# Wide attention as one pipeline over four passes, with whole fp32 scores and the softmax division ahead of the transpose

## What is computed

```python
qkv = (x @ w_qkv).reshape(b, n, 3, HEADS, DIM_HEAD)      # HEADS 16, DIM_HEAD 64, n 256
q, k, v = transpose(qkv, (2, 0, 3, 1, 4))
sim  = einsum('bhid,bhjd->bhij', q * DIM_HEAD ** -0.5, k)
attn = softmax(sim, axis=-1)
out  = einsum('bhij,bhjd->bhid', attn, v)
return merge_heads(out) @ w_out
```

## Time and profile before

| what | us |
|---|---|
| time, median of 3 (2217.66 to 2232.74) | 2226.12 |
| the profiled execution, its own time | 2226.03 |
| its span, first to last instruction | 2224.2 |
| its mean granted TensorE clock | 0.962 of 2.4 GHz |

### The profile page before, as it was taken

How to read it: one execution, slowest core, us unless ns; L and a number is a source line. 1 busy time by engine, 2 the same in 40 slices (tenths; PEclk the granted TensorE clock), 3 DMA queues, 4 the chain that set the end, 5 groups by cost and what they waited for, 6 DMA issues and landing times. The chain is left out here.

```text
span 2224.2 us, 25438 instructions
## 1 busy us (share of the span) xinstructions
PE 1951.9 (88%) x8468; PEld 1143.5 (51%) x8468; DVE 1607.6 (72%) x3009; ACT 893.5 (40%) x1871; POOL 563.4 (25%) x497
## 2 busy tenths in 40 slices
PE   5779999999999989988988789987888887888998
PEld 2346657777776755556766545542232232224555
DVE  4868875454545468866665588857999999996887
ACT  2125444343434354534544523334434353333322
POOL 2633220000000022221011000005767777760000
PEclk9989999999999989999999999988999999999999
DMA  5000000000000000010000000000000000000000
GB/s 221 1 0 1 1 1 1 1 1 1 1 1 1 1 1 1 1 38 1 1 1 1 1 0 1 0 0 15 3 12 1 15 1 15 1 0 0 1 1 19
DMA packets 9633, 20.20 MB, mean 9 GB/s; under 512 B 1056, under 2 KB 8224, under 8 KB 8608
## 3 DMA queue, kind: packets, MB, share of 16 engines
q1 hardware_dynamic: 9504, 18.59, 2.5%
HBM read 14.39 MB, written 1.05 MB: 7 GB/s over the span
## 5 line engine op out<-in xcount | busy, mean ns | idle before, releaser
L1773 POOL TENSOR_TENSOR ssm_hc<-ssm_h,ssm_cm 128x512 f32<-128x512 f32 x256 | 334.3, 1307 | 135.3 <-DVE ssm_h L1856 134.7
L1856 DVE TENSOR_TENSOR_SCAN ssm_h<-banks,ssm_dbx 128x512 f32<-128x512 f32 x256 | 309.6, 1210 | 2.3 <-DVE ssm_dbx L1848 2.3
L515 PE MATMUL banks<-ffn_x_high,up_high 128*128 128x512 f32 x544 | 289.3, 532 | 5.8 <-DVE ffn_p L1489 2.5
L1657 PE MATMUL banks<-ssm_hc,const 128*128 128x512 f32 x512 | 267.4, 604 | 12.2 <-DVE ssm_gated L1831 9.3
L550 POOL TENSOR_TENSOR x_norm<-x_centred,x_square 128x512 f32<-128x512 f32 x24 | 32.8, 1367 | 921.9 <-ACT x_square L545 921.4
L1748 ACT ACTIVATE banks<-banks,a_neg 128x510 f32<-128x510 f32 x256 | 167.2, 659 | 242.5 <-PE banks L1644 241.5
L516 PE MATMUL banks<-ffn_x_low,up_high 128*128 128x512 f32 x544 | 218.5, 402 | 0.0
L517 PE MATMUL banks<-ffn_x_high,up_low 128*128 128x512 f32 x544 | 218.4, 401 | 0.0
L1467 ACT ACTIVATE ffn_th<-banks 128x512 f32<-128x512 f32 (+1 forms) x136 | 81.2, 597 | 273.2 <-PE banks L517 228.2
L1848 DVE TENSOR_TENSOR ssm_dbx<-banks,ssm_bm 128x512 f32<-128x512 f32 x256 | 170.7, 667 | 19.2 <-PE banks L1647 18.6
L1644 PE MATMUL banks<-ssm_packed,half 96*128 96x510 bf16 x256 | 101.7, 397 | 71.8 <-DVE ssm_h L1856 64.7
(11 more groups left out here) (259 smaller groups left out, 3824.7 us busy)
## 6 DMA issues: line engine op xcount, KB each, us to landing
ssm_packed<-ssm_parts SPq DMA_DIRECT2D x48, 64.0 KB, 2.0
up_whole<-in_up SPq DMA_DIRECT2D x1, 2304.0 KB, 16.0
weights<-in_weights SPq DMA_DIRECT2D x1, 2048.0 KB, 21.4
up_whole<-in_up SPq DMA_DIRECT2D x1, 2048.0 KB, 7.9
const<-in_const SPq DMA_DIRECT2D x1, 1426.5 KB, 6.6
half<-in_half SPq DMA_DIRECT2D x1, 1408.0 KB, 10.1
weights<-in_weights SPq DMA_DIRECT2D x1, 1168.0 KB, 23.9
weights<-in_weights SPq DMA_DIRECT2D x1, 1152.0 KB, 11.2
```

Source lines behind the costliest of these rows:

```text
L515: pe.matmul(out, w_high, x_high, start=True, stop=False)
L1657: pe.matmul(k.bank[5][:], k.c("hot")[:, P - row:2 * P - row], hc[:, i % HOLD, :], start=(i % NP == 0), stop=(i % NP == NP - 1)).then_inc(s ...
L1773: pool.tensor_tensor(hc[:, i % HOLD, :], h[:, i % HOLD, :], cm[:, i // NP % 2, :], ALU.mult) \
L1856: dve.tensor_tensor_scan(h[:, n % HOLD, :], k.bank[DELTA[n % AHEAD]][:], dbx[:, n % AHEAD, :], 0.0, ALU.mult, ALU.add).then_inc(s["h"], 1)
```

## The change

`wide_attention` takes all four passes in one list of 64 slots.

- q and k are stored whole, in fp32, by ACT alone. `scores` makes one fp32 product for each t and m, t outside, so that neighbours in the list are of different heads.
- The exponential also writes the sum of each row (`den`). DVE takes the reciprocal (`invert`), and POOL multiplies `pin` by it in place, four instructions a slot (`rden`, `scaled`). `turn` waits for that. `pin` and the small tiles are threefold (`RING`).
- DVE makes both copies into `pt`.
- `weigh` has the operands exchanged: `va` without its 65th column is stationary (64 columns), `pt` moves (256 columns), and the two heads write partitions 0 to 63 and 64 to 127 of bank 6. So the result is channel by token and isn't transposed again. ACT copies it once per pair of slots into `ot`.
- `output(p)` is eight products in a row, in slot 2 of the next pass, ahead of `turn` there; `weigh` comes behind it in that slot and waits for the residual.
- PE's order in a slot is scores, projection, weigh, then norm or v product, then turn. The v products lie in slots 3 to 6 and 11 to 14 (four before the first slot), all copied by DVE from bank 7. The norm of the next pass lies in slots 7 and 8.

```diff
-def wide_attention(k, n, p):
+def wide_attention(k, tag):
...
     nc = k.nc
-    G, HP, tag = 2, H // 2, f"{n}p{p}"
-    s = k.semaphores(f"attend{p % 2}", ATTEND)
+    G, HP = 2, H // 2
+    NS = HP * NB
+    ALL = PASSES * NS
+    RING = 3
+    s = k.semaphores("wide", ["proj", "moved", "v", "v_in", "scores", "max", "probs", "rden", "scaled", "turned",
+                              "pt", "pv", "ot", "y", "done"] + PREP)
...
-        q, kk = ([sb(f"{name}_{part}", [P, 2, T], F32R) for part in ("high", "low")] for name in "qk")
-        va = sb("va", [P, NT, H, DB + 1])
-        pin = sb("pin", [P, 2, 2, T])
+            return ctx.enter_context(nc.sbuf_tensor(f"wide_{name}", shape, dt))
+        q, kk = sb("q", [P, 2, T]), sb("k", [P, 2, T])
+        va = sb("va", [P, NT, H, DB])
+        pin = sb("pin", [P, RING, 2, T])
         pt = sb("pt", [P, 2, 2, T])
-        low = sb("low", [P, 2, 4])
-        rden = sb("rden", [P, 2, 2])
-        on = sb("on", [P, NT, H, DB])
-        ot = sb("ot", [P, 2, T])
+        low, den, rden = sb("low", [P, RING, 4]), sb("den", [P, RING, 4]), sb("rden", [P, RING, 4])
...
-        out = k.bank[6][:, 0:4 * (DB + 1)].rearrange("p (t m e) -> p t m e", t=2, m=2)
...
             def scores(i):
-                g, b = stages[i]
-                pe.wait_ge(s["k_low"], g + 1)
+                p, g, b = pair_of(i)
+                pe.wait_ge(s["moved"], 2 * (i // 2) + 2)
                 if i >= 2:
                     pe.wait_ge(s["probs"], i - 1)
                 else:
-                    pe.wait_ge(s["v_act"], NT)
-                    pe.wait_ge(s["v_dve"], NT)
-                for m in range(2):
-                    r = slice(64 * m, 64 * m + 64)
-                    for t in range(2):
-                        ins = cut_product(pe, k.bank[2 * (i % 2) + m][:, t * L:(t + 1) * L],
-                                          [part[r, g % 2, b * L + t * P:b * L + (t + 1) * P] for part in q],
-                                          [part[r, g % 2, b * L:(b + 1) * L] for part in kk])
+                    pe.wait_ge(s["v_in"], 4)
+                r = i // 2 % 2
+                for t in range(2):
+                    for m in range(2):
+                        rows = slice(64 * m, 64 * m + 64)
+                        ins = pe.matmul(k.bank[2 * (i % 2) + m][:, t * L:(t + 1) * L],
+                                        q[rows, r, b * L + t * P:b * L + (t + 1) * P],
+                                        kk[rows, r, b * L:(b + 1) * L], start=True, stop=True)
                 ins.then_inc(s["scores"], 1)
             def turn(i):
-                pe.wait_ge(s["probs"], i + 1)
+                pe.wait_ge(s["scaled"], i + 1)
                 if i >= 1:
-                    pe.wait_ge(s["pt_act"], i)
-                    pe.wait_ge(s["pt_dve"], i)
+                    pe.wait_ge(s["pt"], i)
                 for m in range(2):
                     for key in range(2):
                         for t in range(2):
                             ins = pe.transpose(k.bank[4 + m][:, key * L + t * P:key * L + (t + 1) * P],
-                                               pin[:, i % 2, m, t * L + key * P:t * L + (key + 1) * P], k.c("ident"))
+                                               pin[:, i % RING, m, t * L + key * P:t * L + (key + 1) * P], k.c("ident"))
                 ins.then_inc(s["turned"], 1)
...
             def weigh(i):
-                g, b = stages[i]
-                pe.wait_ge(s["pt_act"], i + 1)
...
-                for m in range(2):
-                    for t in range(2):
-                        for key in range(2):
-                            ins = pe.matmul(out[:, t, m, :], pt[:, i % 2, m, key * L + t * P:key * L + (t + 1) * P],
-                                            va[:, 2 * b + key, 2 * g + m, :], start=(key == 0), stop=(key == 1))
+                p, g, b = pair_of(i)
+                pe.wait_ge(s["pt"], i + 1)
+                pe.wait_ge(s["v_in"], 8 * p + 4 * (g // 4) + 4)
+                if b == 0 and i >= 2:
+                    pe.wait_ge(s["ot"], i // 2)
+                if i % NS == 0 and p >= 1:
+                    pe.wait_ge(s["done"], p)
+                for key in range(2):
+                    for m in range(2):
+                        ins = pe.matmul(k.bank[6][64 * m:64 * m + 64, b * L:(b + 1) * L], va[:, 2 * b + key, 2 * g + m, :],
+                                        pt[:, i % 2, m, key * L:(key + 1) * L], start=(key == 0), stop=(key == 1))
                 ins.then_inc(s["pv"], 1)
-            for i in range(NS + 2):
-                if i < NS:
+            def output(p):
+                pe.wait_ge(s["ot"], HP * (p + 1))
+                for g in range(HP):
+                    ins = pe.matmul(k.bank[6][:], k.w(G, "wout")[:, g * P:(g + 1) * P], ot[:, g, :],
+                                    start=(g == 0), stop=(g == HP - 1))
+                ins.then_inc(s["y"], 1)
...
+                p, at_slot = i // NS, i % NS
+                if i < ALL:
                     scores(i)
-                    if i + 3 < NS:
-                        project((i + 3) // 2, (i + 3) % 2)
-                if 1 <= i <= NS:
+                if i + 3 < ALL:
+                    project(i + 3)
+                edge = i >= NS + 2 and (i - 2) % NS == 0
+                if edge:
+                    output(p - 1)
+                elif i >= 2:
+                    weigh(i - 2)
+                if at_slot == 7 and p + 1 < PASSES:
+                    norm(p + 1, 0)
+                if at_slot == 8 and p + 1 < PASSES:
+                    norm(p + 1, 1)
+                if 11 <= at_slot < 15 and p + 1 < PASSES:
+                    values(8 * (p + 1) + at_slot - 11, 7)
+                if 3 <= at_slot < 7 and p < PASSES:
+                    values(8 * p + 4 + at_slot - 3, 7)
+                if 1 <= i <= ALL:
                     turn(i - 1)
-                if i >= 2:
+                if edge:
                     weigh(i - 2)
...
         @block.scalar
         def _(act):
             act.wait_ge(k.loaded, 16)
...
+                part, r = (q, kk)[n % 2], n // 2 % 2
+                act.wait_ge(s["proj"], n + 1)
+                if n >= 4:
+                    act.wait_ge(s["scores"], 2 * (n // 2) - 2)
+                act.activation(part[:, r, :], k.bank[7][:], ACT.Copy,
+                               scale=float(DB) ** -0.5 if n % 2 == 0 else 1.0).then_inc(s["moved"], 1)
...
+                if i + 3 < ALL:
+                    move(i + 3)
+                if i < ALL:
                     act.wait_ge(s["max"], i + 1)
-                    if i >= 2:
-                        act.wait_ge(s["turned"], i - 1)
+                    if i >= RING:
+                        act.wait_ge(s["turned"], i - RING + 1)
                     for m in range(2):
                         for t in range(2):
-                            cols = slice(t * L, (t + 1) * L)
-                            ins = act.activation(pin[:, i % 2, m, cols], k.bank[2 * (i % 2) + m][:, cols], ACT.Exp,
-                                                 bias=low[:, i % 2, 2 * m + t:2 * m + t + 1])
+                            cols, n = slice(t * L, (t + 1) * L), 2 * m + t
+                            ins = act.activation(pin[:, i % RING, m, cols], k.bank[2 * (i % 2) + m][:, cols], ACT.Exp,
+                                                 bias=low[:, i % RING, n:n + 1],
+                                                 accum_out=den[:, i % RING, n:n + 1])
                     ins.then_inc(s["probs"], 1)
...
+                if at_slot == 7 and p + 1 < PASSES:
+                    prepare_scalar(k, act, s, p + 1, 0)
+                if at_slot == 8 and p + 1 < PASSES:
+                    prepare_scalar(k, act, s, p + 1, 1)
+                if i >= 2 and i % 2 == 1:
+                    pair = (i - 2) // 2
+                    act.wait_ge(s["pv"], i - 1)
+                    if pair >= HP:
+                        act.wait_ge(s["y"], pair // HP)
+                    act.activation(ot[:, pair % HP, :], k.bank[6][:], ACT.Copy).then_inc(s["ot"], 1)
...
+        @block.gpsimd
+        def _(pool):
+            prepare_gpsimd(k, pool, s, 0)
+            for i in range(ALL):
+                pool.wait_ge(s["rden"], i + 1)
+                for m in range(2):
+                    for t in range(2):
+                        n, part = 2 * m + t, pin[:, i % RING, m, t * L:(t + 1) * L]
+                        ins = pool.tensor_scalar(part, part, rden[:, i % RING, n:n + 1], 1.0, ALU.mult, ALU.mult)
+                ins.then_inc(s["scaled"], 1)
+                if i % NS == 8 and i // NS + 1 < PASSES:
+                    prepare_gpsimd(k, pool, s, i // NS + 1)
...
+            def invert(i):
+                dve.wait_ge(s["probs"], i + 1)
+                dve.reciprocal(rden[:, i % RING, :], den[:, i % RING, :]).then_inc(s["rden"], 1)
+            for j in range(NT):
+                values(j, j)
```

(17 more changed lines are left out.)

## The result

| what | before | after |
|---|---|---|
| time, median, us | 2221.9 | 2139.35 |
| lowest to highest, us | 2215.97 to 2232.74 | 2135.41 to 2140.0 |
| span of the profiled execution, us | 2224.2 | 2133.6 |

The ratio is 0.962, with a 95% interval of 0.958 to 0.966: the change makes the kernel 3.8% faster; the medians lie 83 us apart. The forecast was 2127, in a range from 2104 to 2178.

What follows compares the result with a forecast made beforehand. PE bounded the layer (423 of 449 us busy); afterwards the ring would bound plain slots, PE those with v. Head, slots, v products, norms, edges and tail gave 344.5 us, plus clock 349.5 against 448.6: 2127 us, range 2104 to 2178.

Steps and rivals of the forecast that it cites:

- 63 steps at the plain slot: Steps from first to last turn in the wide attention layer, each taken at 4.25 us: 267.8 us.
- 28 v products, beyond a plain slot: Slots with an added v product, taken at 4.85 us, 0.60 more than a plain slot: 16.8 us.
- norms: The next pass's norm woven into the slots, holding back the projection by some 1.7 us a pass: 5 us in all.
- three edges: At each pass edge the output products stand before turn and weigh waits for the residual: 7.0 us each, 21.
- last turn to the end: The layer's tail: transposes, copies, last weigh, eight output products and residual, 12.2 us.
- clock: Mean clock of 0.97 loses some 10 us of PE work in the layer, half of it counted: 5 us.
- Scores and weigh: On PE, half arrays overlap fully in both products: 0.87 us each per slot, against 1.75 if serial.
- the prediction's first rival: Weigh's column halves do not overlap, so PE takes 0.88 us more a slot: 45 us more, 2172; chance 0.15.
- The ring: Loop of turn, two copies, reciprocal, POOL's scaling and turn sets plain slots: sum 4.10 us, taken as 4.25.
- POOL is the bound: POOL's 256 columns cost 0.61 us, making the ring 5.27 us: 42 us more, 2169; chance 0.12.
- PE's length: PE's own work per slot, products plus four switches of 0.09 us: 3.93 us, or 4.79 with a v product.
- the fourth rival: Waiting PE is held at 1.2 GHz; all through, the layer takes 282 us more, 2409; chance 0.05.

Runs made afterwards that it cites:

- half of POOL's work: The changed kernel with POOL scaling only the first head of each pair, the second left undivided: 2122.9 us, 0.956 of the kernel before.
- the experiment with constants: The changed kernel with POOL multiplying by the constant 1.0 instead of the reciprocal, four instructions of 256 columns: 2125.6 us, 0.957 of the kernel before.
- shared: The changed kernel with POOL scaling the first head and DVE the second, nothing left out: 2128.6 us, 0.958 of the kernel before.
- constants in four and in two: The changed kernel with POOL multiplying by a constant, in four instructions of 256 columns (2125.6 us) or two of 512 (2122.5 us).

## Why the prediction was right, and where it was 10 us short

The sign, the mechanism and the order of sizes held. The layer was put at 349.5 us and took 359.7. By the prediction's own terms:

| term | forecast, us | measured, us |
|---|---|---|
| head to the first score | 15.2 | 14.8 (325.34 to 340.09) |
| first score to first turn | 6.5 | 6.9 |
| 63 steps at the plain slot | 267.8 | 282.9 (63 x 4.49) |
| 28 v products, beyond a plain slot | 16.8 | 16.0 (28 x 0.57) |
| norms | 5 | 3.4 (6 x 0.57) |
| three edges | 21 | 19.4 (3 x 6.46) |
| first distance longer, by the clock | 0 | 1.3 |
| last turn to the end | 12.2 | 15.1 (669.92 to 684.99), 3.0 of it by the clock |
| clock | 5 | 4.3, in the two rows above |

**Scores and weigh.** Right: both overlap wholly, and serialized, each costs 39 to 41 us, where the prediction's first rival had 45. A doubt that was given 0.15 fell.

**The ring.** Right as the bound of plain slots, and half of POOL's work moves it to PE's length. Its size was missed: copies 1.21 (1.22 forecast), reciprocal and hand-over 0.26 (0.26), turn 1.13 (1.1), POOL 1.84 where 1.44 was taken. The term that failed is the price of one instruction, "1.0 ns a column and 0.36 for 256", carried from a tensor_scalar with two constants to one with a value per partition. Of the 0.40, 0.33 are that operand by the experiment with constants. The forecast had put 0.15 on top of its sum for hand-overs, so 0.24 a slot came out too short. The rival "POOL is the bound" had the mechanism, at 0.61 an instruction instead of 0.46.

The table's row of 15 us is not all the ring's, though. It counts 4.49 for all 63 steps, and only 25 are plain: 25 x 0.24 = 6 us. Another 25 hold a v product and are PE's, 5.06 where 4.85 was taken: 5 us, in which POOL has no part, since they stay at 5.06 when it multiplies by constants. Slots with a norm (5.06, taken at 5.08) and edges (16.0 for two slots, taken at 16.1) came out at their price. So the 10 us that the layer is over the forecast are in nearly equal parts the ring's and PE's; the clock's terms cancel.

**PE's length.** 3.93 and 4.79 were forecast, 4.16 and 5.06 measured. Scores to projection 1.06 instead of 0.96, projection to weigh 1.06 instead of 1.05, weigh to the next 1.01 instead of 0.96, a v product 0.96 instead of 0.86. The v product, between two other shapes, has a switch of its own, which the sum had left out. In the scores the second pair of passes starts 0.31 us after the first, where the later ones follow in 0.22; that PE waits for its new weights there is argued, not shown. The slots with v were taken at 4.85.

**What became of the split.** The prediction gave no value to the low parts leaving DVE ("worth nothing by themselves"). That is refuted: in the pipeline dropping the split gains 9 us, all of it through bank 7, which DVE's second reading holds for 0.7 us. In the kernel before it gains 23 to 25 us with the new order of the products, of which slots are 64 x 0.18 = 12, which turning the order of the split products would have given as well; the rest is at the starts of the passes and in the clock. What the prediction priced was DVE's time; what counts is the buffer that DVE holds. The step from 1.25 to 0.87 for the scores was credited to the whole products, and the twelve split ones take 0.91 once their order is turned.

**The clock.** The prediction spread 5 us over the layer. The size was right, the place was not. In the pipeline nothing was lost: the mean over 360 to 660 us is 1.00. It was lost at the two ends, after waits of PE: 1.3 us in the first slot (5.76 against 4.49) and 3.0 at the end (15.1 us from the last turn, where the run with half of POOL's work, at 2.4 GHz there, took 12.1, just as forecast). The layer's 0.99 is better than the 0.97 taken, and the fourth rival had no part.

**Norms and edges.** Each norm product costs 0.57 us, no more than a v product does. The square and the copy of ACT, from which a delay was inferred, lie from 378.49 to 379.59 us in the first pass, and the projection behind them starts at 380.10 without a wait.

**The range.** Its lower end, 2106, was added up wrongly. With slots at 3.93 and 4.79 the prediction's own terms give 63 x 0.32 less 28 x 0.26, some 13 us, and not 19. The measured time is far from that end.

The medians of the four kernels with less work on POOL (shared, constants in four and in two, half) lie 11 to 17 us below the changed kernel's, and the distances from the first copy to the last explain 7 to 12 of it (315.7, 314.1, 311.8 and 310.9 us against 323.0). Much of the rest is in the end of the layer, by the clock: from the last turn on they take 14.2, 12.1, 13.8 and 12.1 us, against 15.1. When the clock falls there differs from kernel to kernel, and what decides it stays open, as does the part that each of the overlap, the pipeline and the clock would have alone.

## What to carry to other kernels

When work moves into a ring over several engines, sum the ring by rows of the very form of instruction (operand per partition or constant, size), since a tenth of a microsecond there comes back in every turn. Two heads of 64 channels fill the array together in both directions: as row halves in the scores and as column halves in the product with v, where the stationary side is v and the result comes out already transposed. Before calling an instruction off the bound engine free, look which buffer it holds while it waits its turn. When a comparison changes the form of the products and their order at once, look at a run that has only one of them: here the split products in the new order were the cheapest of all.

## What the runs showed of the hardware

- Two fp32 products that use other column halves of the array and the same 128 rows overlap wholly: eight passes of 256 columns in 1.08 us, against 1.94 in one half.
- Four whole fp32 products in pairs of row halves take 1.06 us to the next start, and 1.07 in the other order. Twelve fp32r ones take 0.91 with neighbours in different halves, and 1.25 in the kernel before, where both products of one half come before those of the other.
- A tensor_scalar on POOL of 256 columns steps by 0.45 us with a value per partition and by 0.37 with constants; two of 512 with constants take 1.20.
- POOL's scaling of SBUF tiles gets slower beside DVE's: two instructions took 1.13 us for 0.94.
- The granted clock fell to 1.2 GHz after waits of PE in an otherwise full stretch: after 2.55 us before the first turn, and after four of 0.9 to 1.4 us at the layer's end. With products put into those waits at the end it stayed at 2.4.
- Reading the sum of an exponential does not lengthen a run of them by its 0.21 us each: four with sums step by 0.45 us (342.81, 343.26, 343.71) where they stepped by 0.37 without.
